# Score columns of a three-layer graph attention kernel on VectorE instead of TensorE, with fillers on TensorE and new orders for the first and last six turns

## The chip, the core and the metric

The kernel runs on one core of a Trainium2 chip. The metric is the device time of one execution in microseconds (us). A core has TensorE (PE in the profile; PEld is its loading of weights), VectorE (DVE), ScalarE (ACT) and GpSimd (POOL), each with a queue of its own that it works through in order; SyncE (SP) and ScalarE also issue the transfers (DMA) between DRAM and on-chip memory. Engines wait for one another through semaphores.

## What is computed

For each of 32 batches (256 nodes, 256 features, a 256 x 256 adjacency) the reference runs a one-head graph attention layer, adds the input and normalises, then runs two more attention layers (four heads of 128, then one of 256), adds and normalises again:

```python
# layer A
Wh = h @ W
e = leaky_relu((Wh @ a1)[:, :, None] + (Wh @ a2)[:, None, :], 0.2)
e = where(adj == 0, -1e9, e)
h_prime = elu(softmax(e, axis=2) @ Wh)
x = layernorm(x + h_prime)
# layers B (4 heads, then elu) and C, each:
xl = (x @ W).reshape(B, N, H, F)
e = leaky_relu(asrc[:, :, None, :] + adst[:, None, :, :], 0.2)
e = where(adj or diagonal, e, NEG_INF)
out = einsum('bsdh,bshf->bdhf', softmax(e, axis=1), xl) + bias
# end
x = layernorm(x + out)
```

The scores need `x @ (W @ a)` for two vectors a per head. The kernel puts the two columns `W @ a` (times 0.8 and -0.8) in front of W's own columns, so that a projection gives the scores along with the values. These "score columns" depend on the weights alone and are made once, at the start.

## The kernel before

Each batch goes through stages: project A, spread (transposing the score column over all partitions), maxima, shift, logit, exp, transposing the attention weights, weighing the values with them, norm, elu, residual, layer norm, transposing x1; then the same for the four heads of B and for C. `project(B)` and `project(C)` use a high and a low part of weights and inputs (`Wh`, `Wl`, `inh`, `inl`), three matmuls for each k tile. The stages are written as small functions, and every engine has a hand-laid list of calls to them: `fill` for the first turns, `body` for one turn of the steady loop, `drain` for the last. The calls of `body` run under `iterations`, 25 times; in one turn five or six batches are under way at different stages (`t1` to `t5`). `fill` and `drain` name the batches b0 to b5 and e6 to e1. The order of the work on an engine is the order of these calls, whatever is ready. A PSUM bank's number stands in a call; TensorE's `take_bank` waits until the bank's last use has been read.

The names that the change touches:

- `load_weights_T` and `load_vectors` load the transposed weights and the vectors. ScalarE's queue begins with waits for the constants, then issues those of A, the vectors, its table load, then B's. SyncE loads C's.
- `scale_vectors` (L845) on VectorE multiplies the vectors by 0.8 and -0.8, `score_products` (L1432) on TensorE forms the columns (8 matmul records for A, 16 for C, 16 for B), and `score_columns` (L850) on VectorE copies them beside W.
- `round_weights` (L537, ScalarE) and `split_weights` (L855, VectorE) make `Wh` and `Wl` of B and C. `spread_b1`, `finish_b1`, `column_sums`, `finish_b2` spread the biases.
- `project_a` (L1465), `project` (L1480), `spread` (L1494), `transpose_weights` (L1505), `weigh` (L1513), `weigh_head` (L1524), `transpose_x1` (L1534) are TensorE's steps. A matmul of f32 operands shows as two records, a transpose as one.
- `maxima` (L899), `top` (L916), `shift` (L927), `logit` (L941), `inverse_sum` (L951), `elu_first` (L963), `low_b` (L972) are VectorE's; `exp` (L558) and `weights_copy` (L577) ScalarE's; `residual`, `rstd`, `normalise`, `scale`, `low_c`, `fix_scores` GpSimd's.
- `warm_up(bank, count)` runs matmuls of `ones` whose result nobody reads.

The first calls of TensorE's fill and the last of its drain, shortened:

```python
warm_up(7, 4)
score_products(A, 6)
project_a(1, 0, b0)
project_a(0, 2, b0)
spread(A, 0, 3, b0)
score_products(C, 4)
...
spread(C, 0, 2, e1)
transpose_weights(C, 0, 5, e1)
weigh(C, 0, 6, e1)
weigh(C, 1, 3, e1)
```

## Time and profile before

| | |
|---|---|
| median of 3 runs | 668.99 us (668.9 to 669.03) |
| profiled execution, its own time | 667.11 us |
| span of the profiled execution, first to last instruction | 665.2 us |
| TensorE busy | 637.9 us (96%) |
| VectorE busy | 588.7 us (88%) |
| ScalarE busy | 482.0 us (72%) |
| GpSimd busy | 448.6 us (67%) |
| mean granted TensorE clock | 0.988 |

Busy time is the time in which an engine has an instruction running; matmuls overlap, so a run of them is best read from start to start. The span is cut into stretches where the engines' load differs.

### The profile page before, as it was taken

The numbers are of one execution on the slowest core, as the hardware profiler recorded it, in microseconds if no ns is written. First come the engines' busy times: TensorE is split into PE (matmuls) and PEld (weight loads), VectorE is DVE, ScalarE is ACT, GpSimd is POOL, SyncE is SP. The second block draws the span as 40 slices with busy tenths as digits, with TensorE's granted clock in tenths as the row PEclk, the third lists the DMA queues.
The fourth block names the chain that finished last, engine by engine and source line by source line (L and its number), as shares of the span: only waits on it lengthen the run. The fifth ranks groups of instructions, "written<-read, shape, count | busy, mean of one in ns | idle before, by whom it ended". The sixth has DMA issues, their size and how long they took to land. (4 is left out here: it accounts for less than half of the span.)

```text
span 665.2 us, 17485 instructions
## 1 busy us (share of the span) xinstructions
PE 637.9 (96%) x4156; PEld 574.9 (86%) x4156; DVE 588.7 (88%) x2315; ACT 482.0 (72%) x1220; POOL 448.6 (67%) x811
## 2 busy tenths in 40 slices
PE   6979999999999999999999999999999999999993
PEld 5758899998999999999999989999999999988871
DVE  1488999999999999999999999999999999899953
ACT  1457887787778777777787777778877777687661
POOL 0247577777777777677777777777777777666762
PEclk9999999999999999999999999999999999999996
DMA  8311112222212222221122222211222222210001
GB/s 269 96 48 36 46 49 80 81 65 81 67 37 75 81 81 80 65 81 62 40 77 81 81 67 78 81 48 50 80 81 80 65 80 73 89 33 0 18 17 47
DMA packets 46693, 45.68 MB, mean 69 GB/s; under 512 B 2817, under 2 KB 46337, under 8 KB 46594
## 3 DMA queue, kind: packets, MB, share of 16 engines
q1 hardware_dynamic: 45648, 43.79, 20.8%
q8 instruction: 35, 0.57, 0.4%
q10 hardware_dynamic: 946, 0.80, 0.4%
q14 instruction: 64, 0.52, 0.3%
HBM read 36.19 MB, written 8.39 MB: 67 GB/s over the span
## 5 line engine op out<-in xcount | busy, mean ns | idle before, releaser
L378 POOL TENSOR_SCALAR probB<-probB,rdenB 128x256 f32<-128x256 f32 x256 | 124.7, 499 | 79.9 <-DVE rdenB L958 79.6
L558 ACT ACTIVATE probB<-probB,shiftB 128x256 f32<-128x256 f32 x256 | 127.1, 499 | 16.8 <-DVE shiftB L927 13.0
L1524 PE MATMUL PS<-probTB,VB 128*128 128x256 f32 x512 | 128.2, 382 | 0.9 <-ACT probTB L577 0.8
L941 DVE SCALAR_TENSOR_TENSOR probB<-PS,VB,gatedB 128x256 f32<-128x256 f32 x256 | 111.5, 478 | 1.8 <-issue 0.4
L389 POOL TENSOR_TENSOR inlC<-hidT,inhC 128x512 fp32r<-128x512 f32 x64 | 82.0, 1281 | 43.7 <-ACT inhC L622 43.6
L899 DVE CUSTOM_DVE_ANT_0 gatedB<-PS,gate_bc 128x256 f32<-128x256 f32 x256 | 93.8, 420 | 7.3 <-PE PS L1494 5.5
L1524 PEld LDWEIGHTS PS<-probTB,VB 128*128 128x128 f32 x512 | 89.3, 190 | 11.0 <-ACT probTB L577 2.1
L1480 PE MATMUL PS<-WhB,inhB 128*128 128x260 f32 x256 | 81.8, 319 | 1.4 <-DVE inlB L972 1.2
L577 ACT ACTIVATE probTB<-PS 128x512 f32<-128x512 f32 x128 | 72.9, 591 | 9.9 <-PE PS L1505 9.6
L360 POOL TENSOR_TENSOR y<-y,xres 128x512 f32<-128x512 f32 x32 | 41.1, 1286 | 52.4 <-DVE y L963 52.4
L1480 PE MATMUL PS<-WhC,inhC 128*128 128x258 f32 x256 | 75.4, 294 | 0.5 <-issue 0.4
L1505 PE MATMUL PS<-ident,probB 128*128 128x128 f32 x512 | 72.4, 273 | 1.4 <-POOL probB L378 1.4
L1480 PE MATMUL PS<-WlC,inhC 128*128 128x258 f32 x256 | 72.5, 283 | 0.0
L1480 PE MATMUL PS<-WhB,inlB 128*128 128x260 f32 x256 | 72.5, 283 | 0.0
L1480 PE MATMUL PS<-WlB,inhB 128*128 128x260 f32 x256 | 72.3, 282 | 0.0
L1480 PE MATMUL PS<-WhC,inlC 128*128 128x258 f32 x256 | 72.3, 282 | 0.0
L1513 PE MATMUL PS<-VC,probTC 128*128 128x257 f32 x256 | 67.3, 389 | 1.7 <-ACT probTC L577 1.7
L1465 PE MATMUL PS<-WA,xTin 128*128 128x258 f32 x256 | 65.4, 397 | 0.3 <-issue 0.3
L1513 PE MATMUL PS<-VA,probTA 128*128 128x257 f32 x256 | 64.7, 393 | 0.0
L1505 PEld LDWEIGHTS PS<-ident,probB 128*128 128x128 f32 x512 | 59.6, 141 | 5.5 <-issue 2.4
L611 ACT ACTIVATE ehid<-PS,minus 128x512 f32<-128x512 f32 x64 | 44.0, 687 | 28.1 <-issue 17.2
L987 DVE TENSOR_TENSOR VB<-PS,b1x 128x260 f32<-128x260 f32 x128 | 54.2, 426 | 10.6 <-PE PS L1480 9.2
(108 smaller groups left out, 1626.1 us busy)
## 6 DMA issues: line engine op xcount, KB each, us to landing
adj_in<-in_adj_dram SPq DMA_DIRECT2D x32, 256.0 KB, 4.3
xTin<-in_x_t_dram SPq DMA_DIRECT2D x32, 256.0 KB, 4.1
adjT_in<-in_adj_t_dram SPq DMA_DIRECT2D x32, 256.0 KB, 3.1
xres<-in_x_dram SPq DMA_DIRECT2D x32, 256.0 KB, 2.8
out_dram<-res SPq DMA_DIRECT2D x32, 256.0 KB, 2.1
WTC<-in_L_gnn_W_t_dram SPq DMA_DIRECT2D x1, 512.0 KB, 7.4
WTB<-in_L_gnn_W_t_dram ACTq DMA_DIRECT2D x1, 512.0 KB, 8.0
WB<-in_L_gnn_W_dram SPq DMA_DIRECT2D x2, 256.0 KB, 8.3
```

Source lines behind the costliest of these rows:

```text
L378: last = pool.tensor_scalar(B.prob[h][:, k, :], B.prob[h][:, k, :], B.rden[:, k, h:h + 1], 1.0, ALU.mult, ALU.mult)
L389: pool.tensor_tensor(C.inl[:, s, :], hidT[:, s, :], C.inh[:, s, :].bitcast(F32), ALU.subtract)\
L558: last = nc.scalar.activation(L.prob[h][:, k, :], L.prob[h][:, k, :], ACT.Exp, bias=L.shift[:, k, h:h + 1], accum_out=den[:, k, h:h + 1] i ...
L577: nc.scalar.activation(L.probT[h][:, :, :], PS[b][:, :].rearrange("p (k n) -> p k n", k=NT), ACT.Copy)\
L899: last = nc.vector.tensor_tensor_reduce(out=L.gated[h][:, k, :], in0=PS[b][:, (h % 2) * N:(h % 2 + 1) * N], in1=gate[:, k, :], scale=0.25, ...
L941: last = nc.vector.scalar_tensor_tensor(out=L.prob[h][:, k, :], in0=PS[b][:, (h % 2) * N:(h % 2 + 1) * N], scalar=L.V[:, k, h, 1:2], in1=L ...
L987: nc.vector.tensor_tensor(B.V[:, tile, hs, :], PS[b][:, 0:2 * (B.F + 2)].rearrange("p (h f) -> p h f", h=2), b1x[:, hs, :], ALU.add).then_ ...
L1465: last = nc.tensor.matmul(PS[b][:, 0:D + 2], xTin[t.at % 2][:, k, tile * P:(tile + 1) * P], A.W[:, k, 0, :], start=(k == 0), stop=(k == A. ...
L1480: last = nc.tensor.matmul(PS[b][:, 0:n * (L.F + 2)], x_[:, k, tile * P:(tile + 1) * P], w_[:, k, n * g:n * (g + 1), :].rearrange("p h f -> ...
L1505: last = nc.tensor.transpose(PS[b][:, o:o + P], L.prob[h][:, q, k * P:(k + 1) * P], ident[:, :])
L1513: last = nc.tensor.matmul(PS[b][:, 0:L.F + 1], L.probT[0][:, k, u * P:(u + 1) * P], L.V[:, k, 0, 2:L.F + 3], start=(k == 0), stop=(k == NT ...
L1524: last = nc.tensor.matmul(PS[b][:, o:o + N], B.V[:, k, h, 2:B.F + 2], B.probT[h][:, k, :], start=(k == 0), stop=(k == NT - 1))
```

## The change

A's, B's and C's score columns are made on VectorE: a product of W's 256 (or a head's 128) columns with the vector, which a DMA has copied to all 128 partitions, with the sum over them written straight beside W. A takes four such instructions, C eight, B sixteen. A's come first in VectorE's queue; most of C's and half of B's follow A's first `shift`, the others stand further back. The transposed weights are no longer loaded, `scale_vectors` and `score_products` are gone, ScalarE's and TensorE's waits at the head of their queues are dropped or moved (the wait for the identity goes to the first `spread`). `warm_up` calls are put between TensorE's first steps and ahead of the last transposes of the drain. The calls of `fill` and `drain` on all five queues are put in a new order with other banks; apart from what is named here they are the same calls. `body` is unchanged on every queue.

```diff
-        def load_weights_T(eng, L):
-            wT = w0T if L is A else w1T if L is B else w2T
-            eng.dma_start(L.WT[:, :, :], wT.rearrange("(q p) k -> p q k", p=P)).then_inc(L.s_wtld, DMA)
-
-        def load_vectors(eng):
-            eng.dma_start(vec[:, :], vectors).then_inc(s_vec, DMA)
+        def load_vectors(eng, L):
+            if L is A:
+                eng.dma_start(A.att[:, :, :], a0.rearrange("(j f) o -> j (f o)", j=2).partition_broadcast(P))\
+                    .then_inc(A.s_attld, DMA)
+            else:
+                for j, v in enumerate((asrc1, adst1) if L is B else (asrc2, adst2)):
+                    eng.dma_start(L.att[:, j, :], v.rearrange("h f -> (h f)").partition_broadcast(P))\
+                        .then_inc(L.s_attld, DMA)
...
@@ sync fill
                 load_weights(sp, A)
+                load_xT(b0)
                 load_adj(b0)
-                load_xT(b0)
-                load_xT(b1)
-                load_weights_T(sp, C)
+                load_adjT(b0)
+                load_weights(sp, C)
                 load_weights(sp, B)
                 load_adj(b1)
-                load_adjT(b0)
+                load_xT(b1)
+                load_adjT(b1)
...
                 load_residual(b4)
+                load_residual(b5)
                 store(b0)
-                load_xT(b5)
-                load_residual(b5)
...
@@ gpsimd drain, its end
                 low_c(1, e1)
                 low_c(0, e1)
-                rstd(C, e3)
-                normalise(C, e3)
-                keep_x1(e1)
-                fix_scores(e1)
                 rstd(C, e2)
                 normalise(C, e2)
+                fix_scores(e1)
                 rstd(C, e1)
                 normalise(C, e1)
...
@@ scalar
             def round_weights(L):
                 act.wait_ge(L.s_wld, (B.KT if L is B else 1) * DMA)
-                act.wait_ge(L.s_wab, 1)
+                act.wait_ge(L.s_wab, 2 * L.KT * L.H)
...
-                load_weights_T(act, A)
-                load_vectors(act)
+                load_vectors(act, A)
+                load_vectors(act, C)
                 load_table()
-                load_weights_T(act, B)
+                load_biases(act)
+                load_vectors(act, B)
...
-            act.wait_ge(s_cst, 6)
-            act.wait_ge(s_cst2, 1)
             fill()
...
@@ vector
-            def score_columns(L, b):
-                dve.wait_ge(L.s_wa, 1)
-                nc.vector.tensor_copy(L.W[:, :, :, 0:2], PS[b][:, 0:2 * L.KT * L.H]
-                                      .rearrange("p (k h j) -> p k h j", k=L.KT, h=L.H)).then_inc(L.s_wab, 1)
+            def score_columns(L, k, heads):
+                dve.wait_ge(L.s_wld, (B.KT if L is B else 1) * DMA)
+                dve.wait_ge(L.s_attld, (1 if L is A else 2) * DMA)
+                for h in heads:
+                    for j in range(2):
+                        v = L.att[:, 1 - j if L is A else j, h * L.F:(h + 1) * L.F]
+                        if L.columns > 1:
+                            dve.wait_ge(L.s_wab, L.columns - 1)
+                        nc.vector.scalar_tensor_tensor(out=L.prod[:, j, :], in0=L.W[:, k, h, 2:L.F + 2],
+                                                       scalar=0.8 if j == 0 else -0.8, in1=v, op0=ALU.mult, op1=ALU.mult,
+                                                       accum_out=L.W[:, k, h, j:j + 1]).then_inc(L.s_wab, 1)
+                        L.columns += 1
...
+                score_columns(A, 0, (0,))
+                score_columns(A, 1, (0,))
                 make_gate_a(b0)
-                scale_vectors()
-                score_columns(A, 6)
-                maxima(A, 0, 3, b0)
+                make_gate_b(b0)
+                maxima(A, 0, 2, b0)
                 top(A, 0, b0)
-                logit(A, 0, 3, b0)
+                logit(A, 0, 2, b0)
                 shift(A, 0, b0)
-                inverse_sum(A, 1, 1, b0)
-                inverse_sum(A, 0, 3, b0)
+                score_columns(C, 3, (0,))
+                score_columns(C, 1, (0,))
+                score_columns(C, 0, (0,))
+                score_columns(B, 0, (0, 1))
+                score_columns(B, 1, (2, 3))
+                inverse_sum(A, 1, 4, b0)
                 make_gate_a(b1)
-                score_columns(C, 4)
-                score_columns(B, 0)
-                make_gate_b(b0)
+                inverse_sum(A, 0, 6, b0)
+                score_columns(B, 0, (2, 3))
+                score_columns(B, 1, (0, 1))
                 elu_first(b0)
-                maxima(A, 0, 6, b1)
+                score_columns(C, 2, (0,))
+                finish_b1(2)
                 stats(A, b0)
+                meanvar(A, b0)
+                split_weights(B)
+                maxima(A, 0, 0, b1)
+                make_gate_b(b1)
                 top(A, 0, b1)
-                meanvar(A, b0)
+                split_weights(C)
+                finish_b2(1)
+                low_b(2, b0)
...
@@ tensor
             pe.wait_ge(s_cst, 6)
-            pe.wait_ge(s_cst2, 1)
...
-                warm_up(7, 4)
-                score_products(A, 6)
-                project_a(1, 0, b0)
-                project_a(0, 2, b0)
-                spread(A, 0, 3, b0)
-                score_products(C, 4)
-                transpose_weights(A, 0, 0, b0)
-                project_a(1, 2, b1)
-                weigh(A, 1, 1, b0)
-                weigh(A, 0, 3, b0)
-                score_products(B, 0)
+                warm_up(2, 8)
+                project_a(0, 0, b0)
+                project_a(1, 6, b0)
+                warm_up(3, 2)
+                spread(A, 0, 2, b0)
+                warm_up(3, 2)
+                warm_up(6, 2)
+                warm_up(6, 2)
+                warm_up(7, 2)
+                transpose_weights(A, 0, 4, b0)
+                weigh(A, 1, 4, b0)
+                weigh(A, 0, 6, b0)
+                project_a(1, 3, b1)
...
-                spread(C, 0, 2, e1)
+                spread(C, 0, 1, e1)
+                warm_up(5, 12)
                 transpose_weights(C, 0, 5, e1)
```

## Rows read from the trace of the kernel before

**Rows 1.** Windows: stretch, its length, busy us of each engine, clock, DMA share, GB/s.

```profile
0.00:9.70 9.70, 3.92 (x16) 3.56 (x16) 0.90 (x5) 1.49 (x2) 1.07 (x11) 1.00 0.77 245
...
33.49:89.00 55.51, 50.73 (x321) 43.46 (x319) 48.40 (x188) 38.02 (x99) 33.38 (x58) 0.98 0.13 39
89.00:567.00 478.00, 477.40 (x3201) 438.16 (x3200) 456.15 (x1804) 374.42 (x952) 348.92 (x625) 1.00 0.23 71
567.00:641.90 74.90, 73.54 (x487) 64.88 (x487) 65.98 (x261) 56.10 (x145) 50.08 (x92) 1.00 0.10 33
641.90:665.20 23.30, 10.49 (x50) 7.70 (x48) 7.94 (x29) 4.14 (x9) 10.27 (x19) 0.74 0.09 34
```

**Rows 2.** Timeline of TensorE when saturated: start us, us, engine, line, what.

```profile
61.58 0.28 PE L1480 MATMUL PS<-WlC,inhC 128*128 128x258 f32 x1
61.70 0.28 PE L1480 MATMUL PS<-WhC,inlC 128*128 128x258 f32 x1
...
556.62 1.91 PE L1465 MATMUL PS<-WA,xTin 128*128 128x258 f32 x8
558.37 1.03 PE L1513 MATMUL PS<-VC,probTC 128*128 128x257 f32 x4
559.23 0.60 PE L1505 MATMUL PS<-ident,probB 128*128 128x128 f32 x4
559.67 0.38 PE L1494 MATMUL PS<-ident,VA 128*128 128x128 f32 x2
```

**Rows 3.** Timeline of all engines, 0 to 34 us: the first chain.

```profile
0.78 0.44 SPq L202 DMA_DIRECT2D WA<-in_L_gnn_W_dram  x1
...
2.00 0.44 ACTq L206 DMA_DIRECT2D WTA<-in_L_gnn_W_t_dram  x1
...
9.76 3.78 PE L1465 MATMUL PS<-WA,xTin 128*128 128x258 f32 x8 [0.30 <-issue]
...
16.59 0.15 DVE L927 SCALAR_TENSOR_TENSOR shiftA<-topA,amaxA 128x2 f32<-128x2 f32 x1
...
19.00 0.60 ACT L577 ACTIVATE probTA<-PS 128x512 f32<-128x512 f32 x1 [1.27 <-PE PS L1505]
...
20.48 2.48 PE L1513 MATMUL PS<-VA,probTA 128*128 128x257 f32 x8
22.13 0.17 DVE L951 RECIPROCAL rdenA<-PS 128x1 f32<-128x1 f32 x1 [5.39 <-PE PS L1513]
...
25.10 0.69 DVE L963 SCALAR_TENSOR_TENSOR y<-e,y 128x512 f32<-128x512 f32 x1
...
32.44 0.69 DVE L972 TENSOR_TENSOR inlB<-PS,inhB 128x512 fp32r<-128x512 f32 x1 [0.29 <-ACT inhB L602]
...
33.56 0.78 PE L1480 MATMUL PS<-WhB,inhB 128*128 128x260 f32 x1
```

**Rows 4.** Transfers: KB each, median us from issue to landing.

```profile
WA<-in_L_gnn_W_dram SPq DMA_DIRECT2D x1, 256.0 KB, 2.8
WTA<-in_L_gnn_W_t_dram ACTq DMA_DIRECT2D x1, 256.0 KB, 4.8
```

**Rows 5.** Timeline of VectorE: two maxima in a row, and C's split.

```profile
38.51 0.42 DVE L899 CUSTOM_DVE_ANT_0 gatedB<-PS,gate_bc 128x256 f32<-128x256 f32 x1
38.86 0.08 DVE L899 DVE_READ_ACCUMULATOR2_ANT amaxB<- 128x1 f32 x1
38.86 0.42 DVE L899 CUSTOM_DVE_ANT_0 gatedB<-PS,gate_bc 128x256 f32<-128x256 f32 x1
...
48.52 1.31 DVE L855 TENSOR_TENSOR WlC<-WC,WhC 128x1032 fp32r<-128x1032 f32 x1
```

**Rows 6.** Windows: one microsecond, columns as in rows 1.

```profile
32.00:33.00 1.00, 1.00 (x4) 0.88 (x4) 0.71 (x2) 0.97 (x2) 0.55 (x2) 0.50 0.00 0
```

**Rows 7.** Timeline of TensorE in the last chain.

```profile
652.81 0.82 PE L1505 MATMUL PS<-ident,probC 128*128 128x128 f32 x4 [3.24 <-ACT probC L558]
654.40 3.77 PE L1513 MATMUL PS<-VC,probTC 128*128 128x257 f32 x8 [0.78 <-ACT probTC L577]
```

More of the change, by code:

```diff
@@ new lines, in fill @@
+                project_a(0, 6, b1)
+                column_sums(1)
+                spread(A, 0, 0, b1)
+                transpose_x1(2, b0)
+                project_a(1, 4, b2)
+                project(B, 1, 1, 5, b0)
+                project(B, 0, 1, 3, b0)
+                project(B, 1, 0, 1, b0)
+                spread(B, 1, 5, b0)
+                transpose_weights(A, 0, 7, b1)
+                project(B, 0, 0, 0, b0)
+                weigh(A, 1, 2, b1)
+                spread(B, 0, 6, b0)
@@ L1734, in drain @@
[L1734 to L1735 removed]
+                transpose_weights(C, 0, 5, e6)
+                project_a(0, 0, e2)
+                weigh(A, 1, 2, e3)
+                spread(B, 0, 1, e4)
+                weigh(A, 0, 6, e3)
+                weigh(C, 1, 5, e6)
+                project_a(1, 4, e2)
+                weigh(C, 0, 0, e6)
+                spread(A, 0, 3, e2)
+                transpose_weights(B, 2, 4, e4)
+                transpose_weights(B, 3, 6, e4)
```

1123 lines of the change are left out of this document (538 added, 585 removed).

## The prediction

> **What bounds the kernel now.** I read the windows first, cut where the work changes: the start, the rest of the fill after B's first projection, the 25 turns of `body`, the drain, and the last chain [rows 1]. The reader is to see two kernels in one. In the 25 turns, 89 to 567 us, TensorE is busy 477.4 of 478.0 us, one turn each 19.12 us; the diff leaves every queue's `body` as it is, so these 478 us stay. What the change can touch is 665.2 - 478.0 = 187.2 us, fill and drain, which together hold seven turns of work. Seven turns at 19.12 us are 133.8 us, so 53.4 us are lost at the two ends, and only these can be won.
>
> How they divide follows from the pace of a saturated TensorE [rows 2]: a `project` matmul every 0.12 us, four transposes in 0.44, one `weigh` (four records) in 0.86, one `project_a` in 0.88 (eight records in 1.75, of two tiles). Counting calls in the listing, the fill holds 12 `project(B)` (six matmuls each), 4 `project(C)` (twelve), 10 `project_a`, 21 weighings, 16 weight transposes, 4 `transpose_x1`, and spreads worth 9.5 groups of four. That is 8.6 + 5.8 + 8.8 + 18.1 + 7.0 + 1.8 + 4.2 = 54.3 us of work, done in 89 us: 35 lost. The drain holds 77.3 us (seven turns at 18.8, the sum of a turn's own calls, less 54.3) in 98.2: 21 lost.
>
> Then the timeline of the fill [rows 3]. TensorE starts real work at 9.76, as soon as VectorE has copied A's score columns, and the first projection of B comes at 33.56. Only 7.9 us of the 54.3 are done by then; so 46.4 us of work are left for the 55.5 us up to 89.0, and the remaining losses are in front: about 26 us. That front is one dependency chain through batch 0. Behind it VectorE is nearly as full as TensorE (48.4 and 50.7 us of 55.5 [rows 1]), so both queues pace that stretch.
>
> **The change part by part.**
>
> *A's columns.* Before: ScalarE's queue, held by the constants, issues the transposed weights at 2.00, they and the vectors take 4.8 us to land [rows 3, 4], VectorE scales, TensorE multiplies, VectorE copies: `project_a` starts at 9.76. After: the waits at the head of ScalarE's queue are gone, so the vector's transfer can leave near 0.8, where SyncE's first one leaves. It lands after 2.8 us at best (as WA did), 4.8 at worst (WTA): 3.6 to 5.6; I take 4.8. Then four products with a sum. The trace has no such instruction; the nearest is the maxima form, also 256 wide with an accumulator read, one every 0.35 us [rows 5]. A lower bound is 0.35 and an upper one 0.42 + 0.08 = 0.50; I take 0.40, and 0.27 for 128 wide (128 elements fewer at the pace of 0.35 for 256, roughly). So four cost 1.6 and A is ready at 6.4, 3.3 us earlier (5.0 to 7.6 by the ends). x's transfer leaves second now and should land by 1.3 + 4.8, before that; adj, now third, is due only at the first maxima. Batch 1's x moves back from fourth to eighth on SyncE's queue: with 3.8 MB up to it, at 245 GB/s [rows 1], it has landed at 16.5, and `project_a` of batch 1 comes after the weighings, past 17; if that cover is gone, only batch 1 waits. `store(b0)` moves behind two residual loads, whose waits end when GpSimd has added batch 3, before the result of batch 0 is there. These moves, the order of the memsets, and TensorE's wait for the identity (now at the first spread, at 10 us) I cost at nothing.
>
> VectorE's fixed cost per instruction with SBUF sources has a rule of its own. The Trainium skill, VectorE: DVE Perf Modes (The TRN2 errata), gives 58 cycles plus the elements at 0.96 GHz, an estimate of 0.33 us for 256 and 0.19 for 128, where the row paces 0.35 with the accumulator read. By it the 28 products cost 7.0 us, by my values 9.1; the forecast uses the latter.
>
> *Projection to exp of batch 0.* 9.76 to 16.7 for shift [rows 3]: the same steps, 7 us. Eight warm-up matmuls (sixteen records, 3.5 us at the pace of the slow level) now run from about 1.6, against eight records before. The eight records of `project_a` took 3.78 us, against 1.91 at 2.4 GHz [rows 2, 3], so the engine was at its 1.2 GHz level. I expect the first projections still at that level and 2.4 GHz soon after, since the fillers keep TensorE working through the gaps. Shift at about 13.0 (6.5 + 3.6 + 2.9).
>
> *The products behind it.* `score_columns` of C (three k) and half of B's, 6 x 0.40 + 8 x 0.27 = 4.6 us, now stand in VectorE's queue between shift and the first `inverse_sum`. Before, VectorE sat idle there for 5.39 us [rows 3], and that idle time is the cover. But the weighing comes sooner too: of the 5.4 us from shift to `inverse_sum` (16.7 to 22.13), 0.8 go because the `project_a` of batch 1 no longer stands ahead of `weigh` (the copy was done at 19.60, `weigh` began at 20.48), and 1.2 through the clock. So the cover is only 3.4 us, and `inverse_sum` starts at 17.7: 1.3 us of the gain is handed back. Before, 3.0 us passed from there to `elu_first` (25.10). Now the gate and the other half of B's products (0.4 + 0.2 + 8 x 0.27) stand ahead of it, about as long: 20.8. From `elu_first` to `low_b` it was 7.3 us, a chain over GpSimd, VectorE, TensorE and ScalarE. C's last products and `finish_b1` hide behind GpSimd's addition; behind the statistics VectorE's queue now holds both `split_weights` (1.3 us each, as [rows 5] shows for C), one maxima, a gate and `finish_b2`, 4.4 us, slightly more than what is left of the chain: I add 0.2, so `low_b` starts at 28.3 against 32.44, and the first projection of B at 29.0 against 33.56: **4.5 us earlier**. With the other ends (0.50 for each product, vectors landing at 5.6) it is 2.5; with the good ends 6.
>
> *TensorE.* 40 products with two columns go, 7 us of its time. Most lay in gaps, so I count nothing more for them; if they were not covered they are part of the 4.5.
>
> *The rest of the fill.* The 9.1 us lost between 33.5 and 89 have a part that goes by itself: the clock was down there, 0.50 at 32 to 33 [rows 6], after a stretch in which TensorE stood idle, and the first projections of B paid for it, some 0.9 us. C's split is moved out of the crowded stretch into the front, 1.3 us of VectorE. The new order of all queues is a permutation of the same calls; what it saves beyond that cannot be read from a trace of the old order. I take 1.0 us in all, between 0 and 5. So the fill ends 5.5 us earlier (2 to 10).
>
> *The drain.* `warm_up(5, 12)`, 24 records at about 0.11 us or 2.6 us, runs while the last chain waits: TensorE stood idle 3.24 us before the last transposes [rows 7]. The last eight records took 3.77 us against 1.91 for eight as wide in the steady stretch [rows 2], so 1.8 us, and 0.2 of the transposes, is what the lower level costs. I take the whole 2.0. If the fillers ran too long they would delay the transposes: spread ends near 649.5, 2.6 us later is 652.2, the transposes are due at 652.8, so 0.6 us of room. The remaining order of the last chain is the same; GpSimd now runs the normalisation of the batch before ahead of `fix_scores` of the last, which I find ready within 0.3 us of its due time. Before 641.9, 69.8 us of work take 74.9: 5 lost, of which a new order may save some; I take 0.5 (0 to 3, and a loss of 1 below). Drain: **2.5 us**.
>
> Sum: 5.5 + 2.5 = 8.0 us. The profiled execution took 667.11 us for its span of 665.2; the median of the runs is 668.99, 1.9 above it. 667.1 - 8.0 = 659.1 for the profiled one, and against the median **661.0**.
>
> **The rivals.**
>
> *The gain ahead is absorbed.* VectorE is 87% busy from 33.5 to 89, and its order is new; if it paces the stretch, an earlier start of B turns into waits there. Then the fill gives 2, the drain 2: 665. For it: 48.4 us of VectorE work; against: two splits and a gate are done earlier. 17%.
>
> *The clock doesn't hold.* The fillers leave TensorE at 1.2 GHz in the last weighings: 2 us less, 663. For it: the transposes and gaps around them; against: before the fall TensorE stood idle 3.24 and 0.78 us [rows 7], now for some 0.6 and 0.8. The Trainium skill, TensorE: Matmul & The Clock Gate (Part 4: PE-mode transpose), says that transposes don't count as busy for the clock; the fillers are ordinary matmuls, but the four transposes stand behind them. By that rule this rival's 663 would come out. 8%.
>
> *The order closes the gaps too.* Fill 9, drain 3.5: 656.5. For it: 9 us of loss between 33.5 and 89 and 5 in the drain; against: the old order already keeps TensorE at 91% there. 17%.
>
> *Slower: the broadcasts come late.* The vectors of B and C are now rows read once for each of 128 partitions, 0.75 MB with ScalarE's table load ahead of B's, in a start that already moves 245 GB/s [rows 1]. VectorE is in order: each product that waits holds `inverse_sum`, `elu_first` and everything behind. At 245 GB/s all 3 MB that are due have arrived at 13 to 14 us, as the first is wanted. From about 22 us on the gain of 8 is eaten; at 26 us the time is 672. Against it: the new transfers replace 1.25 MB of transposed weights with 1.0 MB. 8%.
>
> The Trainium skill, DMA: Bandwidth & Descriptors (Issuing engines are not separate DMA queues), says that transfers of both queues share the 16 engines. This supports counting all bytes together.
>
> *Nothing.* One end's gain, some 4 us, is lost at the other, the drain's new order costing what the fill gives: 669. 7%.
>
> **How the numbers follow.** My forecast has 43%, within 659 to 663.5. The range reaches to the closing of gaps and to absorption: 655.5 to 667, leaving out the slower case, nothing, and tails. 0.2% is 1.3 us, about what a measurement can tell here. Faster: 43 + 17 + 8 + 17 = 85%; same 7%; slower 8%.
>
> **What would show it.** Right: the four products of A end by 6.4, `project_a` starts then; first `inverse_sum` follows the fourteenth product without a gap; first project of B near 29; the first turn of `body` near 83.5, and 25 turns in 478; the last eight weighing records take about 2 us with the granted clock at 1.00. Wrong: products at 0.5 us or more; VectorE waiting on a vector's DMA; the clock at 0.50 after 10 us; `body` turns longer than 19.12; TensorE idle for more than 5 us in the drain before the last chain.

## The result, and the profile after

The changed kernel takes 674.63 us (median of 4 runs, 674.02 to 675.54), the kernel before 668.94 (median of 4): ratio 1.0087, 95% interval 1.0064 to 1.0109. It is 5.7 us slower where 8.0 us faster was forecast, outside the range. The profiled execution took 674.02 us with a span of 672.0, 6.8 above the 665.2 of before. Ratios here and below compare executions in the same state of the chip; one execution of the new-drain kernel that took 3658.93 us is left out.

The windows of the changed kernel, columns as in [rows 1], cut at the same events: the first `project_a`, the first projection of B, the first turn of `body`, the first call of the drain; the last cut leaves the drain a first part as long as that of before.

```profile
0.00:8.08 8.08, 3.42 (x16) 3.26 (x17) 1.54 (x9) 1.49 (x2) 1.07 (x11) 0.98 0.59 180
33.39:90.42 57.03, 49.84 (x323) 42.92 (x323) 49.72 (x188) 38.38 (x101) 31.92 (x58) 1.00 0.15 43
90.42:569.39 478.97, 477.90 (x3202) 438.19 (x3201) 457.26 (x1804) 374.81 (x952) 349.09 (x622) 1.00 0.22 70
569.39:644.00 74.61, 67.43 (x446) 59.57 (x446) 66.85 (x249) 50.83 (x133) 50.00 (x88) 1.00 0.11 33
644.00:672.00 28.00, 18.11 (x116) 14.88 (x114) 11.27 (x41) 9.77 (x22) 11.33 (x23) 0.96 0.08 28
```

The first projection of B starts at 33.39 instead of 33.56: nothing is left of the 4.5 us. `body` begins 1.5 us later (90.42, before 88.96). Its 25 turns take 478.97 us, before 478.26; the first alone takes 19.76 in place of 19.12, and the others keep their pace. The drain is 102.6 us long (672.0 - 569.39) against 98.0, although the last weighings became faster. In its first 74.6 us TensorE is busy 67.4 us, where before it was busy 73.5 of 74.9 [rows 1]. That window is where the drain loses. In all it is 1.5 + 0.7 + 4.6 = 6.8 us.

The timeline of the fill, as [rows 3]:

```profile
5.97 0.43 DVE L849 SCALAR_TENSOR_TENSOR prodA<-WA,attA 128x256 f32<-128x256 f32 x1 [5.04 <-DMA WA<-in_L_gnn_W_dram]
...
8.08 3.50 PE L1458 MATMUL PS<-WA,xTin 128*128 128x258 f32 x8 [3.23 <-DMA xTin<-in_x_t_dram]
...
14.42 0.15 DVE L928 SCALAR_TENSOR_TENSOR shiftA<-topA,amaxA 128x2 f32<-128x2 f32 x1
...
17.07 2.88 PE L1508 MATMUL PS<-VA,probTA 128*128 128x257 f32 x8 [0.78 <-ACT probTA L579]
18.27 0.17 DVE L952 RECIPROCAL rdenA<-PS 128x1 f32<-128x1 f32 x1
...
21.81 0.69 DVE L964 SCALAR_TENSOR_TENSOR y<-e,y 128x512 f32<-128x512 f32 x1
22.64 1.32 POOL L362 TENSOR_TENSOR y<-y,xres 128x512 f32<-128x512 f32 x1 [20.73 <-DVE y L964]
22.75 1.49 DVE L849 SCALAR_TENSOR_TENSOR prodC<-WC,attC 128x256 f32<-128x256 f32 x1
...
24.40 0.80 PE L1441 MATMUL PS<-WC,minus 128*128 128x258 f32 x2 [0.68 <-DVE prodC L849]
...
25.78 1.21 DVE L856 TENSOR_TENSOR WlB<-WB,WhB 128x1040 fp32r<-128x1040 f32 x1
26.04 0.99 POOL L338 TENSOR_SCALAR veA<-mvA 128x2 f32<-128x2 f32 x1 [2.08 <-DVE mvA L1032]
26.27 2.95 PE L1441 MATMUL PS<-WC,minus 128*128 128x258 f32 x6
29.78 0.42 DVE L900 CUSTOM_DVE_ANT_0 gatedA<-PS,gate_a 128x256 f32<-128x256 f32 x1 [2.79 <-PE PS L1489]
...
32.56 0.68 DVE L973 TENSOR_TENSOR inlB<-PS,inhB 128x512 fp32r<-128x512 f32 x1
33.39 0.35 PE L1473 MATMUL PS<-WhB,inhB 128*128 128x260 f32 x1 [1.39 <-DVE inlB L973]
```

Up to `elu_first` (21.81, before 25.10) 3.3 us were won. Then two things to read together. C's last product takes 1.49 us, where its twin at 14.49 took 0.42: it ends just behind GpSimd's addition beside it (22.64 + 1.32 = 23.96). And `column_sums` waits for that column (0.68 us) and then takes 4.8 us, most of it at the lower clock (granted clock 0.70 from 24 to 26 and 0.50 from 26 to 30), with A's spread of batch 1 behind it in TensorE's queue and the maxima behind that in VectorE's (2.79 us idle), ahead of `low_b`. The layer norm of batch 0, which `low_b` needs as well, also lost time: its statistics begin 0.8 us behind the addition (before 0.2), and GpSimd's first small step takes 0.99 us beside the split of `WlB` in place of 0.19. From `elu_first` to the end of the layer norm it is 7.5 us (before 6.0), from there to `low_b` 3.3 (before 1.4). All 3.3 us are gone again.

The timeline of VectorE, GpSimd and TensorE at two places of the drain, and TensorE's waits from 569 to 645 (what it waited for, us in total, times, longest):

```profile
574.03 1.29 POOL L391 TENSOR_TENSOR inlC<-hidT,inhC 128x512 fp32r<-128x512 f32 x1
574.17 1.16 DVE L917 SCALAR_TENSOR_TENSOR topB<-amaxB,VB 128x4 f32<-128x4 f32 x1
...
577.85 0.62 PE L1489 MATMUL PS<-ident,VB 128*128 128x128 f32 x4 [0.92 <-DVE VB L988]
...
608.83 1.15 DVE L917 SCALAR_TENSOR_TENSOR topC<-amaxC,VC 128x2 f32<-128x2 f32 x1
608.86 1.09 POOL L372 TENSOR_TENSOR x1b<-x,b2x 128x512 f32<-128x512 f32 x1
```

```profile
PE PS L1473 <- DVE inlB L973: 2.6, 2, 1.5
PE PS L1489 <- DVE VB L988: 2.0, 4, 0.9
PE PS L1529 <- POOL x L354: 0.9, 1, 0.9
PE PS L1473 <- issue: 0.8, 1, 0.8
PE PS L1508 <- ACT probTC L579: 0.6, 1, 0.6
```

A `top` of 4 or 2 elements, normally 0.17 us, takes about as long as the GpSimd addition that began beside it, and behind the first of them TensorE stands still for 0.92 us. These two meetings are called collisions below. The same window of before has 0.8 us of waits for `inlB` and 0.2 others; here they are 7 us. The last chain:

```profile
658.40 2.84 PE L1448 MATMUL PS<-ones 128*128 128x128 f32 x24
661.72 0.66 PE L1500 MATMUL PS<-ident,probC 128*128 128x128 f32 x4 [0.47 <-ACT probC L560]
663.15 1.97 PE L1508 MATMUL PS<-VC,probTC 128*128 128x257 f32 x8 [0.78 <-ACT probTC L579]
```

This part of the forecast holds: 1.97 us against the 3.77 of [rows 7], as expected. The rival in which the four transposes behind the fillers lose the level did not come.

### The profile page after: what moved, and what is told of

Same layout as the page of the kernel before. It is cut to its first block and busy times, and to the rows that moved or that the text cites. A ratio compares the mean times of both kernels' runs of the same rounds, so it can differ in the third digit from the quotient of the medians.

```text
span 672.0 us, 17568 instructions
## 1 busy us (share of the span) xinstructions
PE 637.7 (95%) x4168; PEld 573.6 (85%) x4168; DVE 604.0 (90%) x2366; ACT 482.7 (72%) x1220; POOL 450.5 (67%) x811
## 5 line engine op out<-in xcount | busy, mean ns | idle before, releaser
L380 POOL TENSOR_SCALAR probB<-probB,rdenB 128x256 f32<-128x256 f32 x256 | 126.7, 508 | 73.4 <-DVE rdenB L959 73.1
L1508 PE MATMUL PS<-VC,probTC 128*128 128x257 f32 x256 | 65.4, 381 | 2.3 <-ACT probTC L579 2.3
L1508 PE MATMUL PS<-VA,probTA 128*128 128x257 f32 x256 | 65.2, 394 | 0.8 <-ACT probTA L579 0.8
```

Source lines behind the costliest of these rows:

```text
L380: last = pool.tensor_scalar(B.prob[h][:, k, :], B.prob[h][:, k, :], B.rden[:, k, h:h + 1], 1.0, ALU.mult, ALU.mult)
L1508: last = nc.tensor.matmul(PS[b][:, 0:L.F + 1], L.probT[0][:, k, u * P:(u + 1) * P], L.V[:, k, 0, 2:L.F + 3], start=(k == 0), stop=(k == NT ...
```

## The experiments

In what follows the drain's length is the span's end less TensorE's first call of the drain, and "old" and "new" are the orders of before and of the change. `body` is the same in all. b28 to b31 are batches 28 to 31, which the calls of `drain` name e4 to e1. Starts and lengths in the tables come from one profiled execution each, and an unchanged fill does not take the same time in each: in the eight kernels that have the fill of before, call for call, `body` starts at 88.96 to 90.70 us in six and at 92.8 in two. So a difference of 1 or 2 us in a start of `body` shows nothing by itself; the ratios are of several executions.

**The two ends apart.** Four kernels: before with the new drain; the changed kernel with the old drain; before with nothing but the warm-up ahead of the last transposes; and the columns on VectorE in the old order.

```diff
 # e3_warm_end, before's drain on TensorE
                 spread(C, 0, 2, e1)
+                warm_up(5, 12)
                 transpose_weights(C, 0, 5, e1)
```

> The kernel before with the changed kernel's drain on all five queues, warm-up calls included; fill and score columns as before. Theory 1 (the new orders lose the time, most of it in the drain): the drain alone is 4 to 5.5 us slower, median near 673.5, with TensorE losing some 5 us more than before between the first projections of the drain and the first projection of B of the last batch, and 2 us given back by the clock in the last chain. Theory 2 (the drain is only late because the fill ends late, and its waits come from that): no more than 1 us slower, or 2 us faster through the warm-ups.

> The changed kernel with the drain of the kernel before (no warm-up calls at the end). Theory 1: 1.5 to 2.5 us slower than before, near 671, all of it there when the first turn of the body has ended. Theory 2: the whole difference of about 5.7 us stays, near 674.5.

> The kernel before with one edit: twelve warm-up matmuls ahead of the last transposes. If the clock holds, the last eight weighing records take about 2 us instead of 3.8 and the whole is 2 us faster, near 667. If the clock falls all the same, or the fillers delay the transposes, no change or up to 1 us slower.

> The kernel before with the score columns made on VectorE (A's first, most of C's and half of B's behind A's first shift, the rest where the old copies stood), no product matmuls, no waits at the head of ScalarE's queue; every other call in the old order, drain as before. Theory 1 (orders and clock, not the columns, cost the time): 1 to 4 us faster than before, 665 to 668, with the first projection of B near 30 us. Theory 3 (the 28 products on VectorE are what costs): the first projection of B no earlier than 33.5 us, and 0 to 3 us slower.

| kernel | ratio (95%) | first project B | body starts | drain's length |
|---|---|---|---|---|
| before | 1 | 33.56 | 88.96 | 98.0 |
| new drain alone | 1.0084 (1.0059 to 1.0110) | 34.58 | 90.20 | 102.6 |
| new fill alone | 1.0012 (0.9995 to 1.0029) | 33.20 | 91.16 | 98.5 |
| warm-up at the end alone | 0.9983 (0.9963 to 1.0002) | 33.74 | 89.44 | 96.1 |
| columns on VectorE, old order | 1.0004 (0.9991 to 1.0018) | 35.72 | 90.10 | 98.5 |

The new drain carries nearly the whole slowdown, with a fill that nobody touched: so it does not come from a late fill. The new fill's own part, 0.1%, is within its interval. The warm-up shortens the old drain by 1.9 us in the profiled execution; its ratio alone does not exclude 1. The 28 products themselves cost nothing measurable: in the old order B's projection starts 2 us later with them, the body 1, and the ratio is 1.0004. But I had expected 1 to 4 us of gain there, and that was wrong too. The shift came at 14.99 us, 1.6 earlier than before, and `elu_first` at 25.72, 0.6 later: from 16 to 22 us the granted clock was 0.50 and the first weighings took 3.43 us (2.48 before), and then the split of `WlB` ran beside the normalisation of batch 0, which took 2.18 us in place of 1.09.

**The fill mended.** From the timeline above: C's last product moves into VectorE's idle time at 18.8, the splits of `WlB` and `WlC` behind the layer norm and behind `low_b`, A's spread of batch 1 ahead of `column_sums`, C's vectors behind the table load, and warm-ups fill the gaps up to the first weighing. First all of it, then parts. The kernel with all of it (e5) holds more than these: maxima, top, logit and shift of batch 1 are pulled ahead on VectorE, its exp and the transposes of its weights on the other two queues, and `finish_b1` and `finish_b2` are put back.

```diff
 # e15_one_product: only this, on VectorE
                 make_gate_a(b1)
+                score_columns(C, 2, (0,))
                 inverse_sum(A, 0, 6, b0)
 ...
                 elu_first(b0)
-                score_columns(C, 2, (0,))
 # e12_fill_apart: this too
-                split_weights(B)
                 maxima(A, 0, 0, b1)
                 make_gate_b(b1)
+                split_weights(B)
                 top(A, 0, b1)
-                split_weights(C)
                 finish_b2(1)
                 low_b(2, b0)
                 make_gate_a(b2)
+                split_weights(C)
 # e14_fill_apart_warm: e12 and, on ScalarE and TensorE
-                load_vectors(act, C)
                 load_table()
+                load_vectors(act, C)
 ...
-                warm_up(2, 8)
+                warm_up(2, 15)
 ...
-                warm_up(7, 2)
+                warm_up(7, 6)
                 transpose_weights(A, 0, 4, b0)
+                warm_up(5, 2)
 # e11_fill_spread: only this, on TensorE, and the values of b1 ahead of round_weights on ScalarE
                 project_a(1, 3, b1)
-                spread_b1(2)
                 project_a(0, 6, b1)
-                column_sums(1)
                 spread(A, 0, 0, b1)
+                spread_b1(2)
+                column_sums(1)
```

> The changed kernel's fill with the drain of before (as in the new-fill run, ratio 1.001), and five moves in the fill, all read from its timeline: C's last product goes into VectorE's idle time at 18.8 instead of beside GpSimd's residual; split_weights(B) goes behind the layer norm of batch 0 and split_weights(C) behind low_b; spread(A, b1) goes ahead of spread_b1 and column_sums (4.8 us); C's vectors leave behind the table load, so that x has the DMA engines; and warm-up matmuls fill the gaps up to the first project_a and around the first transposes. Theory 1 (the fill's gain was lost in the chain of batch 0 itself, by these five): project_a at 7.5, shift 13.2, elu_first 20.3, low_b 28.5 to 29.5 in place of 32.6, first project B at 29.5 to 30.5 in place of 33.2, body start at 88 to 89.5 in place of 91.2, ratio 0.996 to 0.999. Theory 2 (the stretch from 33 to 90 us is paced by VectorE and by the queues' orders, an earlier start is absorbed): first project B as early, but body start within 1 us of 91 and the ratio at 1.000 to 1.002.

> The changed kernel's fill with the drain of before (as in the new-fill run, 1.0012), and of the mended fill only TensorE's and ScalarE's part: spread(A, b1) ahead of spread_b1 and column_sums, the values of b1 ahead of the rounding. If column_sums ahead of the spread is what held batch 0 (VectorE in order, maxima(A, b1) at 29.8 ahead of low_b): low_b at 30.5 to 31.2 in place of 32.4, first project B at 31.3 to 32, ratio 0.998 to 1.000. If it is the collisions and the splits in VectorE's queue: less than 0.5 us.

> The changed kernel's fill with the drain of before, and of the mended fill only VectorE's part: C's last product in the idle time at 18.8, in place of beside the residual; split_weights(B) behind maxima(A, b1) and make_gate_b(b1), in place of beside GpSimd's layer norm; split_weights(C) behind low_b. If the collisions hold batch 0: the layer norm ends 1 us earlier (28.3 in place of 29.3), and low_b, free of one split, starts at 31.2 to 31.6 in place of 32.4; first project B at 32 to 32.4, ratio 1.000. If column_sums ahead of the spread holds it (maxima(A, b1) at 29.8 stays ahead of split B and low_b): low_b not before 32, ratio 1.001.

> VectorE's part of the mended fill (ratio 0.9991) and, added to it, the warm-up matmuls (7 more ahead of project_a, 4 ahead of the first transposes, 2 behind them) and C's vectors loaded behind the table load. If the clock matters in the chain of batch 0: project_a's first pair and weigh at the high level, shift 1.5 to 2 us earlier than in that run (14.9), elu_first at 20.3 in place of 21.8, first project B at 29.5 to 30, body start 88.5 to 89.3, ratio 0.997 to 0.998. If it doesn't: shift 0.5 earlier at most (the transfer alone), ratio 0.999.

> The changed kernel's fill with the drain of before (ratio 1.0012), and one call of VectorE's moved alone: score_columns(C, 2) from behind elu_first (where it ran beside GpSimd's residual and column_sums waited for it) into the idle time at 18.8. If that call's place is the main cost of the fill: column_sums ends near 25 in place of 29, spread(A, b1) and maxima(A, b1) follow at 25 to 26, first project B 1.2 to 2 us earlier than 33.2, ratio 0.999 to 1.000. If the splits are: under 0.7 us earlier, ratio 1.001.

| old drain, new fill with | ratio (95%) | first project B | body starts |
|---|---|---|---|
| nothing (as above) | 1.0012 (0.9995 to 1.0029) | 33.20 | 91.16 |
| spread ahead of `column_sums` | 1.0016 (1.0000 to 1.0032) | 32.47 | 91.22 |
| one product moved | 1.0005 (0.9994 to 1.0017) | 31.68 | 88.80 |
| that and both splits | 0.9991 (0.9977 to 1.0006) | 30.94 | 90.03 |
| that, warm-ups, C's vectors later | 0.9967 (0.9950 to 0.9983) | 29.61 | 88.00 |
| all | 0.9966 (0.9951 to 0.9982) | 29.48 | 88.33 |

The timeline of the fourth of these rows (the product and both splits), VectorE and TensorE:

```profile
19.68 0.42 DVE L849 SCALAR_TENSOR_TENSOR prodC<-WC,attC 128x256 f32<-128x256 f32 x1
...
22.36 0.60 PE L1441 MATMUL PS<-WC,minus 128*128 128x258 f32 x2
...
25.44 0.42 DVE L900 CUSTOM_DVE_ANT_0 gatedA<-PS,gate_a 128x256 f32<-128x256 f32 x1 [0.40 <-PE PS L1489]
...
30.11 0.69 DVE L973 TENSOR_TENSOR inlB<-PS,inhB 128x512 fp32r<-128x512 f32 x1 [1.80 <-ACT inhB L604]
```

The extra moves of e5 brought nothing over the row above it. Against the changed kernel, the product takes 0.42 again, `column_sums` begins 2 us earlier and doesn't wait, the maxima have 0.40 us of idle time ahead of them in place of 2.79, and `low_b` starts 2.4 us earlier. My sizes were wrong here: I had given VectorE's part 0.8 to 1.2 us at the first projection of B and TensorE's order 1.2 to 1.9. The one call brought 1.5 us there by itself, and the spread's place 0.7, of which nothing was left at the start of `body`. Two things come together in the 1.5: with the call moved, `column_sums` started 0.7 us earlier (23.18, in the new fill alone 23.86) and ran at the higher level, 2.7 us in place of 5.2. Whether the wait for the product had brought the clock down was not tried apart. The intervals of neighbouring steps overlap, so at the end only the whole is shown, from 1.0012 to 0.9966, about 3 us; what each step did is read from single timelines. Then the warm-ups:

```profile
7.91 1.98 PE L1458 MATMUL PS<-WA,xTin 128*128 128x258 f32 x8 [0.83 <-DMA xTin<-in_x_t_dram]
...
15.76 1.97 PE L1508 MATMUL PS<-VA,probTA 128*128 128x257 f32 x8 [0.33 <-ACT probTA L579]
```

The first projections take 1.98 us, where the row without warm-ups took 3.78 (the changed kernel 3.50): TensorE is at its level of 2.4 GHz from the start, and the shift comes at 13.11 in place of 14.91. The weighings took 1.97 in that row already (2.88 in the changed kernel), so they owe the warm-ups nothing. The clock column can't be used here: it says 1.00 from 8 to 12 us in both, so the level is read from the durations. x itself lands at 7.91 here and at 7.98 there, and C's vectors leave behind the table load at 1.42 in place of 1.28, so that edit did next to nothing: the 1.8 us at the shift are the clock's. 1.3 of them were left at the first projection of B, with the clock at 0.50 from 28 to 32 us.

**The port.** Do VectorE and GpSimd wait for one another at the on-chip memory (SBUF; PSUM is the memory that TensorE writes)? Behind the end of before stand six phases (0 to 5) of twelve small VectorE instructions, with and without GpSimd beside them.

```diff
 # e8_port, behind drain(); GpSimd in step: 4 additions (p = 1, 2, 3) or 4 tensor_scalar (p = 4, 5)
+                    if p in (0, 1, 4):
+                        nc.vector.scalar_tensor_tensor(out=..., in0=B.amax[:, 0, 0:4], scalar=4.0,
+                                                       in1=B.shift[:, 0, 0:4], op0=ALU.mult, op1=ALU.max)
+                    elif p in (2, 5):
+                        nc.vector.tensor_scalar(..., B.amax[:, 0, 0:4], 4.0, None, ALU.mult)
+                    else:
+                        nc.vector.scalar_tensor_tensor(out=..., in0=PS[0][:, 0:4], scalar=4.0,
+                                                       in1=B.shift[:, 0, 0:4], op0=ALU.mult, op1=ALU.max)
```

> The kernel before, with a measurement behind its end: six phases in which VectorE runs twelve small instructions (128x4) while GpSimd runs nothing (phase 0), four additions of 128x512 with two on-chip inputs (1 to 3), or four tensor_scalar of 128x256 (4, 5). VectorE's have two on-chip inputs in phases 0, 1 and 4, one in 2 and 5, and one in PSUM with one on-chip in 3. If VectorE's wait comes from a port that both engines' two-input operations share: phase 1 has VectorE instructions of about 1.1 us, one or two for each GpSimd addition, and phases 0, 2, 3 and 5 have none above 0.2; phase 4 between, as the scale of 0.93 us slows down itself. If GpSimd's traffic slows VectorE in general: phases 2 and 3 are slow as well.

VectorE's timeline, phases 1 to 5 (each is announced by a COPY), and GpSimd's first two additions:

```profile
664.50 5.27 DVE L1425 SCALAR_TENSOR_TENSOR e<-amaxB,shiftB 128x4 f32<-128x4 f32 x12
664.67 1.26 POOL L532 TENSOR_TENSOR y<-xres 128x512 f32<-128x512 f32 x1 [0.75 <-DVE e L1422]
665.89 1.27 POOL L532 TENSOR_TENSOR x<-xres 128x512 f32<-128x512 f32 x1
669.76 5.25 DVE L1428 TENSOR_SCALAR e<-amaxB 128x4 f32<-128x4 f32 x12
675.00 0.90 DVE L1430 SCALAR_TENSOR_TENSOR e<-PS,shiftB 128x4 f32<-128x4 f32 x12
680.19 1.83 DVE L1425 SCALAR_TENSOR_TENSOR e<-amaxB,shiftB 128x4 f32<-128x4 f32 x12
682.05 1.86 DVE L1428 TENSOR_SCALAR e<-amaxB 128x4 f32<-128x4 f32 x12
```

With GpSimd idle such instructions follow one another every 0.07 us. Beside four additions of 1.26 us twelve of them take 5.27: four last 1.23 each in place of 0.15, until an addition ends, and one more slips in before the next begins. GpSimd isn't slowed. With one operand in PSUM there is no wait (0.90). I had expected the form with one on-chip input to be free as well; it isn't (5.25). Beside GpSimd's one-input `tensor_scalar` of 0.40 us the waits are about as long as those (0.37 and 0.39 for the two forms). The Trainium skill, SBUF — State Buffer (SBUF: two separate sides), calls the shared pair of ports "an exclusive lock, not a bandwidth split", taken for the whole instruction; GPSIMD Engine Reference (Specifications) names VectorE instructions with two SBUF inputs or in a 2-port perf mode. The trace agrees on the two-input form and on the length of the wait; that the one-input form waits as well fits the second clause, though the trace does not show an instruction's mode.

**The drain mended.** Four tries on before with the new drain. The first takes the two collisions apart; the second, without that, moves the A stages of batches 30 and 31 up in all four engines' queues, 46 calls, some with another bank; the third, in place of that, closes up batch 31's A stage alone behind its first weighing; a fourth adds to the third a freed GpSimd queue.

```diff
 # e6_apart, VectorE
+                elu(0, 6, e5)
                 top(B, 1, e4)
 ...
-                top(C, 0, e4)
                 stats(C, e5)
                 low_b(5, e2)
+                top(C, 0, e4)
 # GpSimd
-                diagonal(e3)
                 low_c(1, e5)
+                diagonal(e3)
 ...
                 scale(2, e2)
-                scale(3, e2)
                 residual(e1)
+                scale(3, e2)
 # e9_b31_behind: e6_apart and, on TensorE (VectorE's inverse_sum, ScalarE's norms alike)
                 weigh(A, 0, 4, e1)
+                weigh(A, 1, 6, e1)
                 project(B, 0, 0, 7, e2)
                 project(B, 1, 0, 2, e2)
                 transpose_weights(C, 0, 5, e4)
-                weigh(A, 1, 6, e1)
 # e13_gpsimd_freed: e9 and, on GpSimd
                 rstd(C, e5)
+                diagonal(e1)
 ...
                 low_c(1, e2)
+                rstd(C, e4)
+                normalise(C, e4)
```

> The kernel before with the changed kernel's drain (as in the new-drain run, ratio 1.0084), and four calls moved by a place or two, so that VectorE's instructions with two on-chip inputs no longer meet GpSimd's additions: elu ahead of top(B, b28), top(C, b28) behind low_b, low_c(1) ahead of diagonal(b29), residual(b31) ahead of scale(3, b30). Theory A (contention of VectorE and GpSimd makes the new drain slow): the two waits of 1 us in the tops go, project B of b31 starts 2 to 3 us earlier than 629.7, ratio 1.004 to 1.005. Theory B (the new order has the A stages of b30 and b31 late in all queues): less than 1 us, ratio 1.007 to 1.009.

> The kernel before with the changed kernel's drain, in which the A stage of b30 and b31 (projection, spread, maxima to exp, transposes, weighing, norm, elu, residual, layer norm, transposing x1) and the first two project(B, b31) are moved up by 3 to 8 us in all queues, with other banks where the old one is taken. Theory B (b31's A stage is late by its place in the queues, and the end lies 41 us behind the first project B of b31): that project starts at 624 to 626 in place of 629.7, and the end follows it, ratio 1.000 to 1.003. Theory A (contention), or a third one (the work left, 24 us of TensorE at project B of b31, sets the end): project B of b31 starts earlier, but the end moves less than 1.5 us, ratio 1.006 to 1.008.

> The kernel before with the changed kernel's drain, with the three moves that took the two collisions out (they brought 2.1 us at TensorE, of which 0.7 was given back where scale(3, b30) fell behind the residual), and the A stage of b31 closed up behind its first weighing only: weigh(A, 1) and inverse_sum(A, 1) directly behind those of half 0 (inverse_sum(A, 1) stood 2.0 us behind the end of its weighing), norms and elu ahead of exp(B, 3, b30), residual ahead of scale(3, b30), whose transposes go behind weigh_head(2, b30). Theory A+B (the drain's loss is two collisions of 1.0 us and some 3 us of waiting of b31's A stage in the queues): project B of b31 at 625 to 626.5 in place of 629.7, ratio 1.002 to 1.004. If the second part is wrong (whatever is moved up pushes back something that is as late, as in the run in which all A stages went up): project B of b31 at 627.5 or later, ratio 1.005 or more.

> The kernel before with the changed kernel's drain, the collisions taken apart and b31's A stage closed up (as in the run before, ratio 1.0058), and GpSimd's queue freed for batches 30 and 31: diagonal(b31) into an idle time at 613, the layer norm of C for b28 behind low_c(1, b30), keep_x1(b31) near the end, scale(0, b30) ahead of fix_scores(b29); on ScalarE the copy of b28's C weights ahead of exp(B, 2, b30). If GpSimd's queue holds the last batches: the scalings 0 and 1 of b30 end 1.2 us or more earlier, the stalls before project B of b31 (1.7), spread(B, 0, b31) (1.3) and project C of b30 (0.9) shrink to under 1.5 together, ratio 1.002 to 1.004. If the order of VectorE and TensorE holds them: less than 1 us, ratio 1.005 to 1.007.

| before, new drain with | ratio (95%) | drain to first project B of b31 | drain's length |
|---|---|---|---|
| nothing | 1.0084 (1.0059 to 1.0110) | 61.5 | 102.6 |
| collisions apart | 1.0062 (1.0043 to 1.0082) | 60.2 | 101.3 |
| A stages of b30, b31 up | 1.0210 (1.0178 to 1.0243) | 65.2 | 111.9 |
| collisions apart, b31 closed up | 1.0058 (1.0037 to 1.0078) | 59.0 | 101.2 |
| that, GpSimd freed | 1.0051 (1.0038 to 1.0064) | 60.1 | 101.1 |
| old drain | 1 | 56.1 | 98.0 |

TensorE's waits in 75 us of the drain, collisions apart:

```profile
PE PS L1505 <- POOL probB L378: 2.0, 1, 2.0
PE PS L1480 <- DVE inlB L972: 1.5, 1, 1.5
PE PS L1494 <- DVE VB L987: 1.0, 3, 0.7
PE PS L1480 <- issue: 0.8, 1, 0.8
PE PS L1513 <- ACT probTC L577: 0.6, 1, 0.6
```

Set call against call, the first collision's removal brings every call of TensorE's 1.0 us forward from the spread of b28 on, the second's another 1.0: by `project(B, b30)` it is 2.1 us. Where `scale(3, b30)` now stands behind the residual, TensorE waits 2.0 us for it, and 1.4 are left at the end. So the collisions' price at TensorE is shown, and it is a third of the loss. The two ratios' intervals overlap; the timelines carry this verdict. The 46 moved calls cost 9 us more instead of saving 4: the spreads then waited 4.6 us for B's values and TensorE 3.1 us for scalings, which fits calls moved up in front of others that were as late. Closing up b31 moved its first projection by 1.1 us and the end not at all: the spread of the same batch waited that much longer. Freeing GpSimd changed nothing at the end. The other two thirds come with the new order and its banks too, since nothing else of weight differs from the old drain, but no single call was found that brings them back: which steps cost them stays open.

**The best of both.** The mended fill, the old drain with the warm-up, and one wait more, so that the split of `WlB` doesn't run beside GpSimd's normalisation of batch 0, which it had stretched from 1.09 to 2.35 us.

```diff
             def split_weights(L):
                 dve.wait_ge(L.s_round, 1)
+                if L is B:
+                    dve.wait_ge(A.s_ln, 1)
```

> The mended fill with the drain of before (ratio 0.9966), the twelve warm-up matmuls ahead of the last transposes (0.9983 by themselves, -1.9 us at the last weighings), and split_weights(B) waiting for the end of GpSimd's normalisation of batch 0, which took 2.35 us beside it in place of 1.09. Additive: -2.3 -1.2 and -0.5 to -1.3 us for the split: ratio 0.993 to 0.995; first project B at 28.1 to 28.8 in place of 29.5. If the fill's head start is absorbed from here on, the split's part is 0 at body start: 0.995.

664.16 us, ratio 0.9933 (0.9911 to 0.9955). Its windows from the first projection of B on, for comparison with those above:

```profile
29.23:86.65 57.42, 49.51 (x321) 42.62 (x319) 50.06 (x188) 36.83 (x98) 32.77 (x58) 1.00 0.15 43
...
565.91:640.80 74.89, 73.38 (x486) 64.61 (x485) 65.93 (x260) 56.09 (x146) 49.87 (x92) 1.00 0.11 33
640.80:662.30 21.50, 11.43 (x75) 9.53 (x74) 7.86 (x30) 4.35 (x9) 10.28 (x19) 0.95 0.11 40
```

The extra wait let the normalisation take 1.38 us (24.37 to 25.75), but the first projection came only 0.25 us earlier (29.23, where I had expected 28.1 to 28.8): `column_sums` now ended at 26.86, at the slow level, and the transposes of x1 (their start overlaps its end) came at 26.66, 0.9 us after the normalisation.

## Why the prediction was wrong, point by point

- **The bound.** Right: apart from 0.6 us in its first turn `body` stayed at its pace, everything else happened at the ends.
- **A's columns at 6.4.** They were ready at 7.4: the products pace 0.35 us, below the 0.40 taken (0.21 for 128 wide, below the 0.27), but W of A took 5.2 us to land in place of the 2.8 of [rows 4]. Three transfers of vectors now leave within the first 2.2 us beside it (which of them held it was not tried apart). The sum had asked only when the vector lands. x landed at 8.08, not before 6.1, so `project_a` came 1.7 us late.
- **Shift at 13.0.** 14.42: those 1.7 less 0.3, with the first projections at the slow level as expected (3.50 us for eight records).
- **`inverse_sum` at 17.7, without a gap behind the fourteenth product.** 18.27, without a gap: right. `elu_first` at 20.8: 21.81, 0.6 of it carried over and 0.4 lost where the clock fell again, the weighings taking 2.88 and VectorE idle for 1.20 us ahead of the second.
- **`low_b` at 28.3.** This is the first step that failed: "From `elu_first` to `low_b` it was 7.3 us", and behind it "I add 0.2". It was 10.75. (From there to the first projection of B the sum gave 0.7 us without saying why, before it was 1.1; it became 0.8.) I had added up VectorE's busy time in that stretch and asked whether it fits; I had not looked at who stands behind the last product (`column_sums`, then the spread, then the maxima ahead of `low_b`), nor at which of VectorE's instructions would run beside GpSimd's. "C's last products and `finish_b1` hide behind GpSimd's addition" was the reverse of what the runs show: the second product took 1.49 us beside it. Nor had I allowed for a clock that falls: `column_sums` took 4.8 us here and 2.7 where the clock stayed up. Moving that one product brought 1.5 us back, the mended fill 3.7 at the first projection of B.
- **The rest of the fill, 1.0.** -1.6: from the first projection of B to the body the changed kernel took 57.0 us, before 55.4. The eight kernels with the new fill, mended or not, took 57.0 to 59.1 there, the nine with the old order 54.4 to 56.1, and the first turn of `body` took 19.7 to 19.8 us in the eight and 19.1 in the nine. The trace of the changed kernel has one wait behind the first projection of B that no old fill has:

```profile
47.26 0.40 PE L1489 MATMUL PS<-ident,VA 128*128 128x128 f32 x2 [2.24 <-DVE probB L942]
```

  It is `spread(A, 0, 6, b2)`. Its input is there at 45.79, but its bank 6 is the one that the last `logit(B, 1, 6, b0)` reads until 47.17, behind the statistics of batch 1 in VectorE's queue. So 1.5 of the 2.24 us hang on a bank's number, which the prediction did not price at all. No run gave it another bank, so what that would bring at the start of `body` is not shown.
- **The drain's clock, 2.0.** Right: 1.9 in the old drain.
- **The drain's order, "0.5 (0 to 3, and a loss of 1 below)".** This is the step that decided: it lost 6.5 us (4.6 of length and the 1.9 that the clock gave). The order was costed as a permutation that could hardly lose, since the calls are the same. Two collisions of 1.0 us were to be read off, had the two queues been laid beside each other; of the other two thirds the runs show only that they come with the new drain, whichever fill stands ahead. Two signs that the prediction had named for being wrong did appear: the clock at 0.50 after 10 us, and more than 5 us of idle TensorE in the drain (7.2 in its first 74.6).
- **The rivals.** None held it. The nearest was "Nothing", which has the drain's new order cost what the fill gives; the fill gave nothing, and the drain's order cost 6.5 us where that rival has some 4. The slower rival, late broadcasts, did not happen: no product of B or C waited for its vector.

## What to carry to other kernels

A new order of the same calls is not free of cost until it is shown to be: in a queue that is nearly full, lay the new lists of two engines beside each other and ask of each moved call who stands behind it, and, for VectorE and GpSimd, whether both will have on-chip operands at that moment. Run the two ends of a kernel apart, with everything else as it was: one such pair of runs placed nearly the whole loss here, and moving a few calls and adding matmuls in idle time then won some 4 us against before, where the large reordering had lost 5.7. What a mended call wins is read at the next event that everything passes: 1.1 us at b31's first projection was 0 at the end, and 0.7 us at B's first projection was 0 at the start of `body`. And ask of each new bank number who still reads that bank.

## What the runs showed of the hardware that was not expected

- VectorE waits for a whole GpSimd instruction even for a few elements and with one on-chip operand: one that lasts 0.15 us lasted 1.23 beside an addition of 1.26, but 0.14 with one operand in PSUM. The wait goes the other way as well: a normalisation by GpSimd took 2.35 us with the split of `WlB` beside it, 1.09 in the kernel before.
- The granted clock differs from run to run in an unchanged fill, and its length with it. Here are the windows of 28 to 36 us in two kernels with the old fill, before and e9_b31_behind (granted clock in the third column from the end):

```profile
28.00:36.00 8.00, 7.11 (x33) 5.48 (x32) 5.52 (x15) 2.10 (x4) 5.22 (x10) 0.79 0.36 108
```

```profile
28.00:36.00 8.00, 8.00 (x18) 4.16 (x18) 3.28 (x13) 1.57 (x3) 3.52 (x8) 0.50 0.45 140
```

The second granted the 1.2 GHz level all through, did 18 matmuls where the first did 33, and had its first projection of B at 38.22 in place of 33.56, the body at 92.8 in place of 89.0. So the starts of `body` of two single profiles compare to some 4 us only, which is why the drains above are compared by their length.
